# A diffusion block on one core: sixteen images pipelined one by one instead of four in lockstep

## The reference

```python
m = silu(mod) @ w_ada + b_ada                      # 9 x 256 per image: shifts, scales, gates
h = _ln(x) * (1 + sc_msa) + sh_msa
h = _self_attn(h, ...)                             # one window of 128 tokens, softmax, @ w_so + b_so
x = x + h * g_msa
h = _ln(x) * (1 + sc_mca) + sh_mca
q = h @ w_q; k, v = split(context @ w_kv)
scores = q.k / 4
top_s, top_i = jax.lax.top_k(scores, 16)           # per head and query, of 128 keys
h = (softmax(top_s) @ v[top_i]) @ w_co + b_co
x = x + h * g_mca
h = _ln(x) * (1 + sc_mlp) + sh_mlp
u = h @ w_m1 + b_m1; h = (silu(u[:1024]) * u[1024:]) @ w_m2 + b_m2
x = x + h * g_mlp
# second layer: x and context normalised, scaled by silu(t) @ Wss + bss,
# full attention of 128 queries on 128 keys, x + out @ Wp + bp
```

## Time and profile before

| | us |
|---|---|
| median of 2 runs | 999.73 (995.76 and 1003.7) |
| the profiled execution's time | 998.08 |
| its span | 996.2 |
| TensorE busy | 792.8 (80%) |
| VectorE busy | 667.5 (67%) |
| ScalarE busy | 513.2 (52%) |
| GpSimd busy | 502.1 (50%) |
| mean granted TensorE clock | 0.916 of full speed |

### The profile page before, as it was taken

The page is one execution under the profiler, slowest core; times in us unless marked ns, Lnnn a source line. Parts: engine busy times, 40 slices in busy tenths (PEclk is TensorE's granted clock), DMA queues, the critical chain, the costliest instruction groups (busy, mean ns, idle before and its releaser), DMA issues.

```text
span 996.2 us, 21054 instructions
## 1 busy us (share of the span) xinstructions
PE 792.8 (80%) x5919; PEld 587.8 (59%) x5919; DVE 667.5 (67%) x2576; ACT 513.2 (52%) x2068; POOL 502.1 (50%) x576
## 2 busy tenths in 40 slices
PE   4869677788879865898887967778898886589987
PEld 3546446676646543676664645657665664377764
DVE  2348888855546888875445688886545689888543
ACT  1258334455558543355565844435565864335556
POOL 3246656544336655554443665455433665556344
PEclk9789789799999976989999988799999997898999
DMA  7351000000000100000000100000000000000000
GB/s 268 110 178 33 17 25 15 18 23 17 27 26 20 31 22 17 22 10 28 24 15 23 29 17 24 16 22 22 17 23 27 12 12 12 12 7 7 1 7 17
DMA packets 33860, 31.15 MB, mean 31 GB/s; under 512 B 7613, under 2 KB 29363, under 8 KB 33475
## 3 DMA queue, kind: packets, MB, share of 16 engines
q1 hardware_dynamic: 33731, 29.66, 10.0%
HBM read 21.20 MB, written 2.15 MB: 23 GB/s over the span
## 4 chain that ended last, share of the span: by engine, by line
PE 40%; DVE 36%; issue 10%; ACT 5%; POOL 3%; SPq 2%; DMA 2%; DVEq 1%; POOLq 0%; ACTq 0%
PE dense_bank L897 10%; PE score_bank L939 7%; DVE left L646 6%; DVE left L657 6%; DVE top L640 5%; DVE top L652 4%; PE dense_bank L904 4%; PE turn_bank L926 4%; PE dense_bank L866 4%; ACT probs L573 3%; PE dense_bank L875 3%; PE o_bank L956 3%; DVE ln_stats L677 2%; PE dense_bank L878 2%; PE dense_bank L884 2%
## 5 line engine op out<-in xcount | busy, mean ns | idle before, releaser
L573 ACT ACTIVATE probs<-score_bank,neg_max 128x128 f32<-128x128 f32 x768 | 272.2, 372 | 254.4 <-DVEq L650 168.7
L939 PE MATMUL score_bank<-k_blocks,q_t 128*128 128x512 f32 x384 | 216.1, 651 | 10.8 <-issue 6.3
L484 POOL TENSOR_TENSOR probs<-probs,row_sum 128x512 f32<-128x512 f32 x128 | 133.1, 1047 | 67.0 <-DVE row_sum L783 66.7
L573 ACT ACTIVATION_READ_ACCUMULATOR probs<-score_bank,neg_max 128x1 f32 x768 | 161.4, 210 | 0.0
L567 ACT COPY probs_t<-turn_bank 128x512 f32<-128x512 f32 x192 | 113.2, 590 | 89.1 <-PE turn_bank L926 80.2
L897 PE MATMUL dense_bank<-h_t,w_m 128*128 128x128 f32 x1024 | 134.4, 293 | 12.2 <-DVEq L694 11.5
L897 PEld LDWEIGHTS dense_bank<-h_t,w_m 128*128 128x128 f32 x1024 | 128.5, 207 | 21.1 <-ACT h_t L533 10.8
L435 POOL TENSOR_SCALAR ln_var<-ln_mv 128x1 f32<-128x1 f32 x80 | 15.2, 190 | 228.3 <-DVE ln_mv L680 226.6
L492 POOL TENSOR_SCALAR left<-left 128x512 f32<-128x512 f32 x64 | 95.5, 1492 | 68.7 <-DVE left L657 68.0
L852 PE MATMUL dense_bank<-ident,x_norm 128*128 128x128 f32 x128 | 32.2, 340 | 107.4 <-DVEq L712 54.0
L777 DVE TENSOR_REDUCE neg_max<-score_bank 128x4 f32<-128x512 f32 x128 | 87.2, 682 | 25.3 <-PE score_bank L939 22.0
(11 more groups left out here) (110 smaller groups left out, 1424.8 us busy)
## 6 DMA issues: line engine op xcount, KB each, us to landing
k_blocks<-k_t SPq DMA_DIRECT2D x384, 16.0 KB, 1.8
gates<-gates_dram SPq DMA_DIRECT2D x16, 384.0 KB, 3.4
k_blocks<-in_L_xcond_w_ada SPq DMA_DIRECT2D x3, 768.0 KB, 9.3
x_in<-in_x SPq DMA_DIRECT2D x16, 128.0 KB, 2.2
ctx_in<-in_ctx SPq DMA_DIRECT2D x16, 128.0 KB, 2.7
w_m<-in_L_xcond_w_m SPq DMA_DIRECT2D x1, 2048.0 KB, 11.9
out_y<-x_mid SPq DMA_DIRECT2D x16, 128.0 KB, 1.7
w_m<-in_L_xcond_w_m SPq DMA_DIRECT2D x1, 1024.0 KB, 13.7
```

The source lines that it names most:

```text
L484: nc.gpsimd.tensor_tensor(probs[:, u % 4], probs[:, u % 4], row_sum[:, u % 4].unsqueeze(2).broadcast_to([P, QH, P]), ALU.mult).then_inc(we ...
L573: e = nc.scalar.activation(probs[:, t % 4, h], score_bank[t % SCORE_BANKS][:, P * h:P * h + P], ACT.Exp, bias=neg_max[:, t % 4, h:h + 1], ...
L939: nc.tensor.matmul(score_bank[u % SCORE_BANKS][:], q_t[:, r, c], k_blocks[:, r, c, blk:blk + 4].rearrange("p h t -> p (h t)"), start=True, ...
```

## The change

The kernel is written anew around one image. Each engine gets a fixed list of parts, each with a lag: in window `n` a part works on image `n - lag`. There is no hardware loop any more; the windows are written out. The lags run up to 22, and the lists begin the first image at lag 16, after the parts that prepare modulations and biases once. In one window an engine so does the SELF part of one image, the CROSS part of one two images older, and the LAST part of one two older again.

- Scores: one burst for all sixteen heads of an image, eight matmuls of 32 partitions by 256 columns. Each strip of 32 partitions holds two heads, and writes to its own one of four banks (`s_bank`). A burst waits until the previous phase's exponentials (and in CROSS its first cuts) are done.
- The maximum is taken over eight heads at a time. The top 16 stays at four heads at a time, but the steps of the four groups are interleaved.
- The softmax division moves behind the value sums for all three attentions: the reciprocals are spread over 256 columns on GpSimd, turned on TensorE, copied by ScalarE and multiplied into the value sums by VectorE. In CROSS the sum is that of the exponentials of the sixteen found values; the matmuls with ones go.
- The mask in CROSS becomes a two-operation scaling that turns the marker into 0 and the rest below -1, an add, and a clamp at zero in ScalarE's copy after the turn.
- The scaling of layer norm moves from VectorE to GpSimd; the evictions of values move from VectorE to ScalarE, their biases being folded into rows made once. Nine of the weight loads are issued from ScalarE's queue.
- All other matmul results, turns included, take turns in three `ring` banks.

The core of the diff:

```diff
-SLOTS = 4
-ITERS = B // SLOTS
-QH = 4
-PHASES = 3 * SLOTS
-UNITS = PHASES * (H // QH)
-SCORE_BANKS, TURN_BANKS, DENSE_BANKS = 3, 2, 2
+XS = 7
+BANKS = 3
+SLOTS = {SELF: 2, CROSS: 2, LAST: 4}
+V_SLOTS = 4
...
+DVE_ORDER = (
+    ("top_a", 0, 20), ("bias", 0, 0), ("silu", 0, 0), ("top_a", 1, 20), ("top_a", 2, 20), ("silu_mul", 1, 21),
...
+def steps(order):
+    lags = [lag for _, _, lag in order]
+    for n in range(B + max(lags)):
+        for name, which, lag in order:
+            b = n - lag
+            if 0 <= b < (1 if name in ONCE else B):
+                yield name, which, b
...
+                if name == "scores":
+                    k, s = which, b % SLOTS[which]
+                    if k == SELF:
+                        pe.wait_ge(qk_ready, b + 1)
+                    else:
+                        pe.wait_ge(q_ready, DVE_N["q", k, b])
+                    pe.wait_ge(k_placed[k, s], 16 * 8 * (b // SLOTS[k] + 1))
+                    before = previous(PHASES, k, b)
+                    if before:
+                        pe.wait_ge(probs_ready, ACT_N["exp", (before[0], 3), before[1]])
+                        if before[0] == CROSS:
+                            pe.wait_ge(left_a, DVE_N["cut_a", 3, before[1]])
+                    q = qk_t[:, b % 2] if k == SELF else q_t[:, k - 1, b % 2]
                     for c in range(CK):
+                        for g in range(4):
+                            rows_g = slice(32 * g, 32 * g + 32)
+                            e = nc.tensor.matmul(s_bank[:, g, C * c:C * c + C], q[rows_g, c],
+                                                 k_blocks[k][rows_g, s, c].rearrange("p e t -> p (e t)"),
+                                                 start=True, stop=True)
+                    e.then_inc(scores_done, 1)
...
+                if name == "mask":
+                    u = which
+                    pool.wait_ge(left_b, DVE_N["cut_b", u, b])
+                    nc.gpsimd.tensor_scalar(left[:, u], left[:, u], -(2.0 ** -126), -2.0,
+                                            ALU.mult, ALU.add).then_inc(mask_done, 1)
+                    pool.wait_ge(probs_ready, ACT_N["exp", (CROSS, u), b])
+                    pool.wait_ge(mask_done, POOL_N["mask", u, b])
+                    nc.gpsimd.tensor_tensor(left[:, u], left[:, u], probs[:, CROSS, u], ALU.add).then_inc(masked, 1)
...
+                if name == "spread":
+                    pool.wait_ge(inv_row_ready, DVE_N["inv", which, b])
+                    nc.gpsimd.tensor_copy(inv_wide[:, which].rearrange("p (h d) -> p h d", d=D),
+                                          inv_row[:, which].unsqueeze(2).broadcast_to([P, H, D])
+                                          ).then_inc(wide_ready, 1)
...
+                    nc.gpsimd.tensor_scalar(x_norm[:, k], src, ln_neg[:, k], ln_rstd[:, k],
+                                            ALU.add, ALU.mult).then_inc(normed, 1)
...
+                if name == "exp":
+                    k, u = which
+                    if k == CROSS:
+                        act.wait_ge(left_a, DVE_N["cut_a", u, b])
+                    else:
+                        act.wait_ge(maxed, DVE_N["max", (k, u // 2), b])
...
+                if name == "o":
+                    k = which
+                    dve.wait_ge(inv_ready, ACT_N["inv", k, b])
+                    dve.wait_ge(o_done, PE_N["sums", k, b])
+                    nc.vector.tensor_tensor(o_t[:, k], o_view, inv_t[:, k], ALU.mult).then_inc(o_ready, 1)
...
+            def take(name, which, b, signal, value):
+
+                n = USE[name, which, b]
+                if n >= BANKS:
+                    pe.wait_ge(*released[n - BANKS])
+                released[n] = (signal, value)
+                return ring[n % BANKS]
```

More of the change, by code:

```diff
@@ L54, in dve_order @@
[L54 to L105, removed]
@@ L134 @@
-KEY_BIAS = {SELF: 28, CROSS: 32, LAST: 36}
+KINDS = range(5)
+HEADS = (SELF, CROSS, LAST)
+GATED = (SELF, CROSS, MLP)
+GATE = {SELF: 0, CROSS: 1, MLP: 2}
+LN_EPS = {SELF: 1e-6, CROSS: 1e-6, MLP: 1e-6, LAST: 1e-5, CTX: 1e-5}
+MOD = {SELF: 0, CROSS: 1, MLP: 2, LAST: 3, CTX: 4}
+NMOD = 4 * len(MOD)
+NBIAS = 60
+NQ_SELF, NQ_CROSS, NQ_LAST, NK_CTX, N_UP, NV = 26, 30, 32, 34, 38, 54
+XS = 7
+BANKS = 3
+SLOTS = {SELF: 2, CROSS: 2, LAST: 4}
+V_SLOTS = 4
+ONCE = {"bias", "silu", "mods", "rows", "last", "weights", "store_rows"}
@@ new lines @@
+SP_ORDER = (
+    ("load_ctx", 0, 18), ("store_rows", SELF, 5), ("load_gates", MLP, 21), ("store_y", 0, 22), ("load_x", 0, 22),
+    ("load_gates", SELF, 19), ("place", SELF, 17), ("store_rows", MLP, 12), ("load_gates", CROSS, 20),
+    ("place", CROSS, 18), ("store_rows", CROSS, 6),
+)
+POOL_ORDER = (
+    ("weights", SELF, 0), ("weights", CTX, 0), ("glu", 0, 21), ("norm", SELF, 17), ("skip", CROSS, 20),
+    ("spread", LAST, 22), ("glu", 1, 21), ("mask", 0, 20), ("mask", 1, 20), ("sub", 0, 20), ("mask", 2, 20),
+    ("mask", 3, 20), ("weights", LAST, 21), ("norm", CTX, 17), ("spread", CROSS, 20), ("norm", LAST, 21),
+    ("weights", CROSS, 19), ("norm", CROSS, 19), ("norm", MLP, 20), ("skip", MLP, 20), ("skip", LAST, 21),
+    ("skip", SELF, 18), ("spread", SELF, 18),
+)
@@ new lines, in steps @@
+def steps(order):
[5 more added lines that the diff above has]
+                yield name, which, b
+BANKED = {"bias", "silu", "mods", "rows", "last", "turn", "qk", "v", "k2", "v2", "q", "T", "inv", "out", "up", "down"}
+USE = {}
+for _part in steps(PE_ORDER):
+    if _part[0] in BANKED:
+        USE[_part] = len(USE)
+PHASES = [(which, b) for name, which, b in steps(PE_ORDER) if name == "scores"]
@@ L137, in block_kernel, with numbered, previous @@
+SUMS = [(which, b) for name, which, b in steps(PE_ORDER) if name == "sums"]
+def numbered(order):
+    seen, number = {}, {}
+    for name, which, b in steps(order):
+        seen[name] = number[name, which, b] = seen.get(name, 0) + 1
+    return number
+POOL_N, ACT_N, DVE_N, PE_N = (numbered(order) for order in (POOL_ORDER, ACT_ORDER, DVE_ORDER, PE_ORDER))
+def previous(phases, kind, b):
+    n = phases.index((kind, b))
+    return phases[n - 1] if n else None
 def block_kernel(nc, a, out):
@@ L233, in block_kernel, with bank @@
+        def bank(name, which, b):
+            return ring[USE[name, which, b] % BANKS]
         cond_loaded = sem("cond_loaded")
[L234 to L235 removed]
         rows_loaded = sem("rows_loaded")
[L237 to L240 removed]
@@ L405, in _ @@
+            for s in range(XS):
+                sp.wait_ge(y_stored[s], 16 * ((B - 1 - s) // XS + 1))
         @block.gpsimd
```

1365 lines of the change are left out of this document (674 added, 691 removed).

## The result

The changed kernel takes **720.83 us** (median of 720.77 and 720.88), the kernel before 999.73. The ratio is 0.721, with an interval of 0.709 to 0.733. The forecast was 772 us with a range from 732 to 852: the direction was right, and the gain of 279 us was 51 us larger than forecast, beyond the range's low end.

What follows compares the result with a forecast made beforehand. No engine was full: images in lockstep made VectorE and TensorE take turns as the bound. First burst at 50, plus 40, fourteen windows of 42 us (588) and 92 gave 770, with 1.9 around it 772 us; range 732 to 852.

Steps and rivals of the forecast that it cites:

- Step 1: All engines: interleaving makes an image cost one window, the larger of the fullest engine's work and the longest ring of waits.
- the ring: Waits through the four score banks, across VectorE, GpSimd, TensorE and ScalarE, closing once per window; 40.3 to 42.9 us.
- the size of a window: Middle of the kernel: 42 us per window, from 39.5 to 47, TensorE's work and the waits for score banks overlapping.
- step 3: Summed the waits through the four score banks from one cross burst to the next: 40.3 to 42.9 us.
- step 2: TensorE's work per window falls from 49.6 to 40.8 us, bounds 38.5 and 46.5, with bursts of 1.75 plus 0.2 tail.
- the rival: Overlapping strip loads, masks at 0.62 us and the upper clock level give a 39.5 us window, 732 us; chance 0.20.
- The fast end: Rival: overlapping strip loads, masks at 0.62 us, upper clock level; window 39.5 us, 732 us in all; chance 0.20.
- Step 4: Other engines per window: VectorE about 34 us, GpSimd 28, ScalarE 32, placing DMAs free; all hidden under 42.
- The ends: Outside the full windows: first score burst at 50 us, windows 18 and 19 about 40, the last four windows 92.
- Serial strips: Rival for TensorE's score bursts: strips of rows run one after another, window 47 us, 852 us; chance 0.13.
- No interleaving: Rival: fixed orders and one set of score banks add waits, TensorE stays 80% full, window 51 us, 916; chance 0.13.
- the slow clock: Rival: waits for score banks keep TensorE at 1.2 GHz, work 75 us per window, 1300 us; chance 0.02.

Runs made afterwards that it cites:

- the serial kernel: Changed kernel with every step of an image issued before any of the next one's, on all engines; 1800 us, ratio 1.798.
- the kernel before without its second eight: Kernel before with the second MAX of the top 16 made a small copy and the second MATCH_REPLACE removed; 945.4 us, ratio 0.946.

## Why the prediction was right in direction and wrong in size

**Step 1 held.** Without the interleaving the same instructions take 1800 us, and with it 171 of the 279 us are there even when the bursts are as slow as full rows. The unit of a window, and the two bounds that a window has, held too: with the ring lowered, another bound takes over within 0.5 us.

**The step that failed is the size of a window, 42 us,** in both of its bounds.

- *Ring, step 3, forecast 40.3 to 42.9, measured 37.5.* One step was not on the ring, and two stretches were priced too high. The cross burst (1.95) lies beside `tanh` and `silu_mul`; in its place stands 0.85 of `silu_mul`: -1.1. VectorE's block took 14.9 instead of 16.3: -1.4. I had priced it from the earlier trace rows, where each step follows on the one that it needs; half of the difference is in the MAX, whose eight groups take 6.3 us on the chain where 8 x 0.88 = 7.0 were put, and the rest in the cuts (0.07 of scaling on the chain, 0.17 in the earlier trace rows) and `silu_mul` (0.59 instead of 0.78). From turn to the end of the LAST burst it took 5.6 instead of 6.5: -0.9, with the burst at 1.08 instead of 1.75, though I had left `out` (L779, 1.0) off. GpSimd's masks took 4.2, and the norms with the spread 4.1, both inside their bounds (4.1 to 5.9 and 3.6 to 4.4). The exps took the forecast 7.8. From the low end of 40.3 that is -1.1 - 1.4 - 0.9 + 0.1 + 0.5 = 37.5.
- *TensorE, step 2, forecast 40.8, measured 0.97 x 37.54 = 36.5.* The 40.8 had two errors of one sign. It used the kernel before's mean clock of 0.916; the middle ran at 1.00, which alone makes 37.4 of it. And a burst occupies TensorE for 0.9 us, not 1.75. Both together would make 37.4 - 3 x 0.85 = 34.8; the other 1.7 us of the 36.5 aren't explained. They may be waits that the rows count as busy, or longer dense matmuls. (The upper bound of 46.5 with bursts of 3.6 us comes to 46.9 by the same sum, which changes nothing.)

**The clock was a result and not a given.** The earlier trace rows had shown 1.00 in a stretch where TensorE was 84% busy, and 0.78 and 0.83 where it was 65%. A window forecast as nearly full of TensorE's work was better priced at 1.00 than at the mean. I used that row only for the rival, and there I made too much of it ("in every stretch where TensorE is over 80% busy"): the earlier trace rows has only this one, and in the stretch just before it TensorE is busy for 87% at 0.92:

```profile
162.00:224.00 62.00, 53.84 (x450) 43.06 (x450) 44.98 (x175) 30.15 (x114) 33.40 (x34) 0.92 0.07 18
```

**Why the low end was too high.** The fast end had all three of its conditions: overlapping loads, masks at 0.63 us, a clock of 1.00. Its 39.5 us still used VectorE's 16.3 and the cross burst on the ring. Range ends were made from unknown prices alone, while the ring itself, as a sum of known rows, was taken as exact.

**Step 4 held.** Per window VectorE comes to 0.84 x 37.5 = 31.6 us (forecast 34), ScalarE to 31.2 (32), GpSimd to 22 to 23 (28; four masks at 0.63 instead of 1.49 us are 3.4 of the difference), all below the bound. The key blocks' DMAs cost nothing once interleaved, and nearly 6 us per self phase when not. The ends came within 2, 6 and 3 us; the first burst waited for DMA for 4.0 us, with 259 GB/s over the first 50 us.

**The rivals.** Serial strips fall: 3.69 us per burst is what full rows take. A burst of about 1.3 us, by which the sum was 758, is near the truth (1.15); what separates 758 from 720.8 lies in the other terms of the ring. No interleaving (916) and the slow clock (1300) fall with 97% at 1.00; the serial kernel shows that the mechanism of the second is real, clock 0.66 at 54% busy. The price of 0.76 us for a change of tiling mode would have added 1.5 us per window to the ring. The chain shows nothing of the kind before the LAST burst, and the rows only 0.17 us of `issue` before its weight loads. The price rested on a misread row: the 0.76 us of the earlier trace rows are idle time of the weight loads, and TensorE's matmuls ran on through it:

```profile
415.31 1.02 PE L939 MATMUL score_bank<-k_blocks,q_t 128*128 128x512 f32 x2
```

TensorE is busy with them until 416.33, and the value sums' own matmuls start at 416.27. Nor did every burst of value sums have it (75 waits in 128 bursts). The Trainium skill (TensorEngine Tiling (Array Packing), Key Properties) has it that changing the tiling mode drains the array; no row here shows such a cost.

## What to carry to other kernels

When a change raises TensorE's share of busy time, price its work at the clock that full stretches of the old trace show, not at the old mean. Ask of each step of a ring whether another branch as long runs beside it. When an instruction's duration varies, look first at whether the long ones end with an instruction of another engine, before putting it down to the step ahead. Two bounds within a microsecond show in three runs: lower each alone, then both; and an engine that is 60% busy still counts nearly in full where the ring runs through it.

## What the runs showed of the hardware

- Weight loads of four strips of rows overlap as the matmuls do: 16 loads of 128 columns in 0.74 us, and 16 score matmul rows in 1.15 us instead of 3.69 for full rows. The order in which strips are issued made no difference (a burst of 1.17 us, 722.9 in all).
- GpSimd takes 0.63 us to multiply and add 128x512 by constants, and 1.49 us to compare the same tile with one.
- A VectorE scaling of 128x4 took 0.15 to 0.17 us in most places. With VectorE's steps group by group it took up to 0.71, and each of the 38 long ones ended with a GpSimd instruction. Over a window, VectorE's order alone was worth 3 us of 37.5.
- The granted clock was 1.00 with TensorE 97% busy and 0.66 with 54%, for the same instructions; in the kernel before without its second eight it was 0.83 in one stretch with 80% and 0.95 in another with 79%.
